# Local attention on TensorE: the value projection moved directly behind the output projection, the transposed inverses behind the scores

## The chip, the cores and the metric

The kernel is one program on one core of a Trainium2 chip. Its engines run their own instruction queues side by side and meet through semaphores: TensorE (matrix products and transposes into PSUM), VectorE (DVE), ScalarE (ACT), GpSimd (POOL) and SyncE (SP), which only issues DMAs here. The metric is the device time in microseconds (us); lower is better. PSUM has 8 banks of 512 fp32 columns per partition, and this kernel uses all of them in local attention.

## The reference

The input is 4 x 512 x 256 x 4 image values and 4 x 512 x 256 text values. An embedding reduces the image to 4 x 512 x 256 and the text is put behind it: 4096 rows of 256. Then comes a layer of linear attention with 16 heads, and then twice a layer of local attention and a gated MLP:

```
h = shift_token(x); q, k, v = split(h @ wqkv)          # 8 heads of 64
q = l2norm(q) * qs; k = l2norm(k) * ksc; q, k = rotary_xpos(q, k)
sim = 8 * q_window @ [k_previous_window, k_window]^T   # windows of 128 rows
attn = softmax(masked sim); o = attn @ [v_previous, v]
x = x + o @ wo                                         # and then the MLP
```

All of it is fp32. The change lies in this part, which runs twice (`local_phase`, `layer` 0 and 1).

## The kernel before

**Windows and stages.** The 4096 rows are 32 windows of 128 (`T`). `schedule` calls `step(n, r, a, b, c, d)` for n = 0 to 34 on each of TensorE, ScalarE and VectorE. Steps 0 to 3 and 32 to 34 are written out; steps 4 to 31 are a hardware loop over pairs of steps (`r` is 0 and 1). Each step works on up to four windows at once: flag `a` is the q and k projection of window n and the input of window n+1, `b` and the scores belong to window n-1, `c` (probabilities transposed, values) to window n-2, `d` (output projection) to window n-3. The order inside a queue is the order of the calls, written out by hand: nothing is reordered.

**Precision.** Projections are three fp32r matmuls, high times high, high times low and low times high (`matmul3`, lines 116 to 118). Operands come as a high part copied by ScalarE and a low part subtracted by VectorE. Transposes are matmuls by the identity.

**TensorE, a step.** `project` of q and k (12 matmuls of 512 columns, L116 to L118); 8 transposes of the rotated q and k (L1170), which wait for `rotated` of POOL; `probs_t` for pairs of heads 0 and 1 (L1133); the output projection (12 matmuls of 256 columns), which waits for `o_done`; `probs_t` for pairs 2 and 3; `project` of v (6 matmuls); `x_t` (L1107, two transposes of the next input); `inverses` (L1152, four transposes of the spread reciprocal row sums); `score` twice (L1126, 16 matmuls); `values` (L1143, 32 matmuls).

**Banks.** `QK, V, TQ, OT = 0, 2, 3, 7`: q and k in banks 0 and 1, v in 2, transposed q and k in 3 and 4, outputs in 7. Scores take banks 0, 1, 3 and 4 again. `XT, RB = 5, 6` and `PT = (5, 6, 5, 6)`: `x_t` shares bank 5 with pairs 0 and 2, `inverses` share bank 6 with pairs 1 and 3. So `x_t` waits for ScalarE's copy of pair 2 (`p_done`), and `inverses` for that of pair 3.

**ScalarE, a step** (L916 to L948): high part of the last output (L920), copy of v (L924), squares of q and k (L928), copies of transposed q and k (L932), four copies of transposed probabilities (`probs_out`, L914), high part of the next x (L896), the input copies (L888 or L889), the copy of the transposed inverses (L945, waits for `r_t`), then the exponentials (L908, eight for a window, each pair waits for `masked`). In the loop there is also one piece of the MLP's weights before each pair of steps (L954).

**VectorE, a step** (L1010 to L1068): in every second step the mask (L1013), the reciprocal of the row sums (L1018, waits for `exped`), the low part of the output (L1022), the rotation (L1030, L1035, waits for `squared`), the residual (L1042), the sums of squares (L1044), small steps for the norm (L998 to L1006), the low part of x (L980, L982), the eight score reductions with mask (L989, wait for `scored`) with more of the small steps between them, and the product of values and inverses (L1068).

**GpSimd**: the sum of the rotated halves (L862), the product by the norm (L866, raises `rotated`), one piece of the MLP's weights in every second step (L876), and the spread of the inverses (L854).

Of the kernel before, what the change touches and what calls it, by code (L numbers as in the profile page):

```python
# [89 lines left out]
class Chain:  # L90
# [16 lines left out]
    def wait(self):  # L107
        self.eng.wait_ge(self.sem, self.base + self.n)
# [5 lines left out]
def matmul3(nc, out, wh, wl, mh, ml, start, stop):  # L114

    nc.tensor.matmul(out, wh, mh, start=start, stop=False, skip_group_check=True)  # L116
    nc.tensor.matmul(out, wh, ml, start=False, stop=False, skip_group_check=True)  # L117
    return nc.tensor.matmul(out, wl, mh, start=False, stop=stop, skip_group_check=True)  # L118
# [646 lines left out]
def local_phase(nc, s, mem, K, A, layer):  # L765
# [29 lines left out]
    QK, V, TQ, OT = 0, 2, 3, 7  # L795
# [17 lines left out]
    with nc.Block() as block:  # L813

        @block.sync
        def _(sp):
            sp.dma_start(flags[:], A.flags).then_inc(s.const_in.sem, 16)
            if layer == 0:
                for dst, src in K.local_loads(layer):
                    sp.dma_start(dst, src).then_inc(K.local_in.sem, 16)  # L820
            for dst, src in ((cos[:], A.rope_cos), (sin[:], A.rope_sin), (prev[:], A.mask_prev),
                             (mask_o[:, P:2 * P], A.mask_cur), (mask_e[:, 0:P], A.mask_cur),
                             (mask_o[:, 0:P], A.mask_prev), (negs[:], A.negs),
                             (qks[:, 0, :], A.ffn_q_scale[layer:layer + 1].to_broadcast([P, DH])),
                             (qks[:, 1, :], A.ffn_k_scale[layer:layer + 1].to_broadcast([P, DH]))):
                sp.dma_start(dst, src).then_inc(s.const_in.sem, 16)
            sp.wait_ge(*s.padded.after(1))
            for dst, src in K.mlp_loads(layer):
                sp.dma_start(dst, src).then_inc(K.mlp_in.sem, 16)
            with sp.Fori(0, T // 2) as p:  # L830
                for r in range(2):
                    sp.wait_ge(*s.y_done.after(2 * p + r + 1))
                    sp.wait_ge(*K.rows_stored[r].after(16 * (layer * T // 2 + p)))
                    sp.dma_start(A.scratch[bass.ds((2 * p + r) * P + 1, P), :].rearrange("(o p) c -> p o c", o=1),
                                 X[:, bass.ds(2 * p + r, 1), P:D]).then_inc(K.rows_stored[r].sem, 16)

            sp.wait_ge(*K.mlp_in.after(16 * len(K.mlp_loads(layer)) * (layer + 1)))
# [264 lines left out]
        @block.tensor  # L1102
        def _(pe):
            def x_t(t, r):
                wait(pe, s.x_copied, t + 1)
                for c in range(KC):
                    last = nc.tensor.transpose(ps[:, XT, c * P:(c + 1) * P],  # L1107
                                               xc[:, r, c * P:(c + 1) * P], K.ident[:])
                last.then_inc(s.x_t.sem, 1)

            def project(r, w, bank):

                cols = slice(w * LINNER, (w + 1) * LINNER)
                for c in range(KC):
                    at = XW * c - c
                    last = matmul3(nc, ps[:, bank], xt[:, r, 0, at:at + P], xt[:, r, 1, at:at + P],
                                   wh[:, c, cols], wl[:, c, cols], c == 0, c == KC - 1)
                return last

            def score(half):  # L1120

                bank = QK if half == 0 else TQ
                for pair in (2 * half, 2 * half + 1):
                    for e in range(2):
                        rows, at = slice(e * DH, (e + 1) * DH), pair % 2 * 2 * P
                        last = nc.tensor.matmul(ps[:, bank + e, at:at + 2 * P], qt[rows, pair, :],  # L1126
                                                kt[rows, :, pair, :], start=True, stop=True)
                last.then_inc(s.scored.sem, 1)

            def probs_t(t, pair):  # L1130
                wait(pe, s.exped, 4 * t + pair + 1)
                for k in range(4):
                    last = nc.tensor.transpose(ps[:, PT[pair], k * P:(k + 1) * P],  # L1133
                                               pm[:, pair, k * P:(k + 1) * P], K.ident[:])
                last.then_inc(s.p_t.sem, 1)

            def values():

                for pair in range(LPAIRS):
                    for w in range(2):  # L1140
                        for e in range(2):
                            h = 2 * pair + e
                            last = nc.tensor.matmul(ps[e * DH:(e + 1) * DH, OT, pair * P:(pair + 1) * P],  # L1143
                                                    vv[:, w, h * DH:(h + 1) * DH],
                                                    pt[:, pair, (2 * e + w) * P:(2 * e + w + 1) * P],
                                                    start=(w == 0), stop=(w == 1))
                last.then_inc(s.o_full.sem, 1)

            def inverses():

                for pair in range(LPAIRS):
                    last = nc.tensor.transpose(ps[:, RB, pair * P:(pair + 1) * P],  # L1152
                                               spread[:, pair * P:(pair + 1) * P],
                                               K.ident[:])
                last.then_inc(s.r_t.sem, 1)

            def step(n, r, a, b, c, d):
                if a or b:
                    wait(pe, s.x_done, n + 1)
                if a:  # L1160
                    wait(pe, s.turned, n)
                    wait(pe, s.masked, 4 * (n - 1) - 2)
                    project(r, 0, QK)
                    project(r, 1, QK + 1).then_inc(s.qk_full.sem, 1)
                if b:
                    wait(pe, s.rotated, n)
                    wait(pe, s.masked, 4 * (n - 1))
                    for k in range(2):
                        for m in range(LPAIRS):
                            last = nc.tensor.transpose(ps[:, TQ + k, m * P:(m + 1) * P], t1[:, k, m * P:(m + 1) * P],  # L1170
                                                       K.ident[:])
                        last.then_inc(s.qk_t.sem, 1)
                if c:
                    probs_t(n - 2, 0)
                    wait(pe, s.r_out, n - 2)
                    probs_t(n - 2, 1)
                if d:
                    wait(pe, s.o_done, n - 2)
                    for m in range(LPAIRS):
                        cols = slice(m * P, (m + 1) * P)  # L1180
                        last = matmul3(nc, ps[:, OT, 0:D], oth[:, cols], otl[:, cols], woh[:, m, :], wol[:, m, :],
                                       m == 0, m == LPAIRS - 1)
                    last.then_inc(s.y_full.sem, 1)
                if c:
                    for pair in (2, 3):
                        wait(pe, s.p_done, 4 * (n - 2) + pair - 1)
                        probs_t(n - 2, pair)
                if b:
                    wait(pe, s.v_done, n - 1)
                    project(1 - r, 2, V).then_inc(s.v_full.sem, 1)  # L1190
                if a:
                    if c:
                        wait(pe, s.p_done, 4 * (n - 2) + 3)
                    x_t(n + 1, 1 - r)
                if c:
                    wait(pe, s.spread, n - 1)
                    wait(pe, s.p_done, 4 * (n - 1))
                    inverses()
                if b:
                    wait(pe, s.qk_done, 2 * n)  # L1200
                    if a:
                        wait(pe, s.turned, n + 1)
                    score(0)
                    score(1)
                if c:
                    wait(pe, s.v_done, n - 1)
                    wait(pe, s.y_done, n - 2)
                    values()

            x_t(0, 0)  # L1210
            if layer == 0:
                pe.wait_ge(*s.w_lo.after(len(PIECES)))
            schedule(pe, step)


# [578 lines left out]
```

## Time and profile before

| | |
|---|---|
| time, median of 3 runs | 2147.8 us (2147.47 to 2151.69) |
| profiled execution | 2146.89 us, its span 2145.1 us |
| TensorE matmuls busy | 1979.4 us (92%) |
| VectorE busy | 1547.7 us (72%) |
| ScalarE busy | 1088.3 us (51%) |
| GpSimd busy | 435.6 us (20%) |
| two windows in layer 0, 1000.30 to 1026.80 | TensorE busy 26.21 us of 26.50, VectorE 24.09, ScalarE 22.05 |

Local attention lies between about 780 and 1240 us (layer 0) and between about 1450 and 1920 us (layer 1). Times in the rows below are microseconds from the start of the span. In a timeline, a row gives the start, the duration, the engine, the line, the operation with its output and inputs, and in brackets the idle time before it with what ended it; neighbours of one kind are merged (x8). Matmuls overlap: their starts tell when the engine takes them, while their durations reach into the next one.

### The profile page before, as it was taken

What the parts mean: (1) busy time and instruction counts of PE and PEld (TensorE: products, weight loads), DVE (VectorE), ACT (ScalarE), POOL (GpSimd) and SP (SyncE); (2) the same over time, 40 slices, a digit from 0 to 9 for tenths busy, and PEclk for the clock granted to TensorE, in tenths of its full rate; (3) what the DMA queues carried; (4) which work ended last, traced back from release to release, by engine and by line L of the source; (5) the groups of instructions that cost most, each with busy time, mean ns of one, the idle gap of its engine ahead of it and who ended that gap; (6) DMA issues with size and microseconds to landing.
All of it is one profiled execution on the core that took longest, in us unless ns stands there. A gap on an engine that the chain in (4) does not pass through costs nothing. (4 is left out here: it accounts for less than half of the span.)

```text
span 2145.1 us, 42708 instructions
## 1 busy us (share of the span) xinstructions
PE 1979.4 (92%) x13792; PEld 1692.4 (79%) x13792; DVE 1547.7 (72%) x4590; ACT 1088.3 (51%) x2517; POOL 435.6 (20%) x265
## 2 busy tenths in 40 slices
PE   8799999899999959999999879995999999959998
PEld 8688788788878847888888668884888888857887
DVE  7356546546636668999998677775899999957777
ACT  5322232232222228888888624443777777743433
POOL 3100000000000014444444200002444444420010
PEclk9899999999999979999999989997999999989999
DMA  8000000000000020000000010001000000000002
GB/s 300 1 1 1 2 1 1 2 1 1 1 2 1 1 105 5 5 5 5 5 5 5 5 61 11 15 5 65 6 5 5 5 5 5 5 16 15 11 10 83
DMA packets 43179, 42.20 MB, mean 20 GB/s; under 512 B 8552, under 2 KB 37959, under 8 KB 43080
## 3 DMA queue, kind: packets, MB, share of 16 engines
q1 hardware_dynamic: 43080, 40.90, 5.8%
q8 instruction: 60, 0.98, 0.2%
q14 instruction: 39, 0.32, 0.0%
HBM read 32.49 MB, written 8.39 MB: 19 GB/s over the span
## 5 line engine op out<-in xcount | busy, mean ns | idle before, releaser
L908 ACT ACTIVATE l_probs<-l_probs,l_negmax 128x256 f32<-128x256 f32 x512 | 253.2, 496 | 65.1 <-DVE l_negmax L989 65.1
L116 PE MATMUL ps<-local_w_hi,l_xT 128*128 128x512 f32 x384 | 167.9, 437 | 37.1 <-DVE l_xT L982 31.2
L862 POOL TENSOR_TENSOR l_t<-l_t,l_t 128x1024 f32<-128x1024 f32 x64 | 152.9, 2388 | 196.3 <-DVE l_t L1035 196.3
L116 PE MATMUL ps<-attn_w_hi,attn_xT_hi 128*128 128x512 f32 x392 | 169.3, 432 | 18.5 <-issue 10.0
L866 POOL TENSOR_TENSOR l_t<-l_t,l_rnorm 128x1024 f32<-128x1024 f32 x64 | 121.9, 1905 | 307.9 <-DVE l_rnorm L1006 307.9
L419 ACT ACTIVATE attn_exp<-ps 128x512 f32<-128x512 f32 x130 | 77.6, 598 | 209.9 <-PE ps L118 209.9
L914 ACT ACTIVATE l_probsT<-ps 128x512 f32<-128x512 f32 x256 | 138.3, 594 | 49.5 <-PE ps L1133 49.5
L117 PE MATMUL ps<-attn_w_lo,attn_xT_hi 128*128 128x512 f32 x392 | 158.5, 404 | 0.0
L118 PE MATMUL ps<-attn_w_hi,attn_xT_lo 128*128 128x512 f32 x392 | 158.0, 403 | 0.0
L510 DVE TENSOR_SCALAR attn_exp<-attn_exp 128x512 f32<-128x512 f32 x130 | 58.8, 453 | 136.6 <-ACT attn_exp L419 136.5
L118 PE MATMUL ps<-local_w_hi,l_xT 128*128 128x512 f32 x384 | 155.4, 405 | 0.0
L117 PE MATMUL ps<-local_w_lo,l_xT 128*128 128x512 f32 x384 | 155.2, 404 | 0.0
L116 PE MATMUL ps<-m_hnT_hi,ffn_w_hi 128*128 128x512 f32 (+1 forms) x352 | 143.1, 407 | 4.6 <-DVE m_hnT_lo L1372 4.6
L117 PE MATMUL ps<-m_hnT_lo,ffn_w_hi 128*128 128x512 f32 (+1 forms) x352 | 140.2, 398 | 0.0
L118 PE MATMUL ps<-m_hnT_hi,ffn_w_lo 128*128 128x512 f32 (+1 forms) x352 | 140.2, 398 | 0.0
L842 POOL MEMSET ffn_w_raw<- 128x44 f32 x2 | 0.3, 136 | 686.6 <-POOLq L384 684.7
L1133 PE MATMUL ps<-ident,l_probs 128*128 128x128 f32 x1024 | 133.9, 274 | 1.7 <-ACT l_probsT L914 1.7
L1126 PE MATMUL ps<-l_kT,l_qT 64*128 64x256 f32 x1024 | 127.9, 389 | 2.5 <-DVE l_t L1035 2.5
L1143 PEld LDWEIGHTS ps<-l_probsT,l_v 128*64 128x64 f32 x2048 | 110.5, 137 | 20.9 <-issue 20.9
L1143 PE MATMUL ps<-l_probsT,l_v 128*64 128x128 f32 x2048 | 125.9, 276 | 0.0
L116 PEld LDWEIGHTS ps<-local_w_hi,l_xT 128*128 128x128 f32 x384 | 74.8, 195 | 61.2 <-DVE l_xT L982 23.8
L1317 ACT ACTIVATE m_gelu<-ps,ffn_b 128x512 f32<-128x512 f32 x80 | 55.0, 688 | 127.7 <-PE ps L118 127.7
(210 smaller groups left out, 5832.2 us busy)
## 6 DMA issues: line engine op xcount, KB each, us to landing
tok_x<-x SPq DMA_DIRECT2D x16, 512.0 KB, 5.6
m_shifted<-shifted SPq DMA_DIRECT2D x20, 256.0 KB, 2.7
shifted<-x SPq DMA_DIRECT2D x64, 64.0 KB, 1.5
out<-x SPq DMA_DIRECT2D x8, 512.0 KB, 4.4
ffn_w_raw<-ffn_w SPq DMA_DIRECT2D x6, 640.0 KB
local_w_raw<-ffn_wqkv SPq DMA_DIRECT2D x4, 768.0 KB, 5.3
h<-txt SPq DMA_DIRECT2D x4, 512.0 KB, 9.6
attn_w_raw<-attn_Wk SPq DMA_DIRECT2D x1, 1024.0 KB, 7.5
```

What stands on the lines that cost most here:

```text
L116: nc.tensor.matmul(out, wh, mh, start=start, stop=False, skip_group_check=True)
L117: nc.tensor.matmul(out, wh, ml, start=False, stop=False, skip_group_check=True)
L118: return nc.tensor.matmul(out, wl, mh, start=False, stop=stop, skip_group_check=True)
L419: nc.scalar.activation(ex[:, at % 2], ps[:, at % 2], ACT.Exp).then_inc(s.attn_exp.sem, 1)
L510: chain(nc.vector.tensor_scalar(ex[:, at % 2], ex[:, at % 2], 1.0, None, ALU.min))
L862: nc.gpsimd.tensor_tensor(t1[:], t1[:], t2[:], ALU.add).then_inc(s.summed.sem, 1)
L866: nc.gpsimd.tensor_tensor(r, r, rn[:].unsqueeze(2).to_broadcast([P, 2 * LH, DH]), ALU.mult).then_inc(s.rotated.sem, 1)
L908: last = nc.scalar.activation(v, v, ACT.Exp, bias=nb[:, h:h + 1], scale=-1.0, accum_out=rsum[:, h:h + 1])
L914: nc.scalar.activation(pt[:, pair], ps[:, PT[pair]], ACT.Copy).then_inc(s.p_done.sem, 1)
L1126: last = nc.tensor.matmul(ps[:, bank + e, at:at + 2 * P], qt[rows, pair, :], kt[rows, :, pair, :], start=True, stop=True)
L1133: last = nc.tensor.transpose(ps[:, PT[pair], k * P:(k + 1) * P], pm[:, pair, k * P:(k + 1) * P], K.ident[:])
L1143: last = nc.tensor.matmul(ps[e * DH:(e + 1) * DH, OT, pair * P:(pair + 1) * P], vv[:, w, h * DH:(h + 1) * DH], pt[:, pair, (2 * e + w) * P ...
```

## The change

In a step of TensorE two blocks move. The wait for `v_done` and the projection of v come directly behind the output projection, ahead of `probs_t` for pairs 2 and 3. The inverses, with their two waits, come behind the two `score` calls, directly ahead of `values`. The other engines' code is as before.

```
                     last.then_inc(s.y_full.sem, 1)
+                if b:
+                    wait(pe, s.v_done, n - 1)
+                    project(1 - r, 2, V).then_inc(s.v_full.sem, 1)
                 if c:
                     for pair in (2, 3):
                         wait(pe, s.p_done, 4 * (n - 2) + pair - 1)
                         probs_t(n - 2, pair)
-                if b:
-                    wait(pe, s.v_done, n - 1)
-                    project(1 - r, 2, V).then_inc(s.v_full.sem, 1)
                 if a:
                     if c:
                         wait(pe, s.p_done, 4 * (n - 2) + 3)
                     x_t(n + 1, 1 - r)
-                if c:
-                    wait(pe, s.spread, n - 1)
-                    wait(pe, s.p_done, 4 * (n - 1))
-                    inverses()
                 if b:
                     wait(pe, s.qk_done, 2 * n)
                     if a:
...
                     score(0)
                     score(1)
                 if c:
+                    wait(pe, s.spread, n - 1)
+                    wait(pe, s.p_done, 4 * (n - 1))
+                    inverses()
                     wait(pe, s.v_done, n - 1)
                     wait(pe, s.y_done, n - 2)
                     values()
```

## Rows read from the trace of the kernel before

**Rows 1.** Stretch of two windows: PE, PEld, DVE, ACT, POOL busy, PEclk, DMA, GB/s.
```profile
1598.53:1625.02 26.49, 26.19 (x219) 22.24 (x217) 24.05 (x80) 20.63 (x58) 11.84 (x7) 1.00 0.02 5
```

**Rows 2.** Waits, 1510 to 1880 us: total us, times, longest.
```profile
PEld ps L1170 <- POOL l_t L866: 16.4, 28, 0.8
```

**Rows 3.** Timeline of TensorE (PE) over two windows of layer 1.
```profile
1594.70 2.00 PE L1126 MATMUL ps<-l_kT,l_qT 64*128 64x256 f32 x16
...
1607.95 2.00 PE L1126 MATMUL ps<-l_kT,l_qT 64*128 64x256 f32 x16
1609.87 1.97 PE L1143 MATMUL ps<-l_probsT,l_v 128*64 128x128 f32 x32
1611.77 0.50 PE L116 MATMUL ps<-local_w_hi,l_xT 128*128 128x512 f32 x1
...
1614.40 0.40 PE L118 MATMUL ps<-local_w_hi,l_xT 128*128 128x512 f32 x1
1614.96 1.09 PE L1170 MATMUL ps<-ident,l_t 128*128 128x128 f32 x8 [0.16 <-POOL l_t L866]
...
1616.68 0.36 PE L116 MATMUL ps<-local_w_hi,l_oT_hi 128*128 128x256 f32 x1
...
1618.18 1.04 PE L1133 MATMUL ps<-ident,l_probs 128*128 128x128 f32 x8
1618.97 0.47 PE L116 MATMUL ps<-local_w_hi,l_xT 128*128 128x512 f32 x1
...
1620.45 0.38 PE L1107 MATMUL ps<-ident,l_x 128*128 128x128 f32 x2
1620.66 0.60 PE L1152 MATMUL ps<-ident,l_spread 128*128 128x128 f32 x4
1621.19 2.00 PE L1126 MATMUL ps<-l_kT,l_qT 64*128 64x256 f32 x16
```

**Rows 4.** Timeline of ScalarE (ACT) in the same windows.
```profile
1596.78 0.51 ACT L908 ACTIVATE l_probs<-l_probs,l_negmax 128x256 f32<-128x256 f32 x1 [1.24 <-DVE l_negmax L989]
...
1600.73 0.45 ACT L954 ACTIVATE ffn_w_hi<-ffn_w_raw  x1
...
1602.08 1.01 ACT L928 ACTIVATE l_sq<-ps 128x1024 f32<-128x1024 f32 x1
...
1610.03 0.51 ACT L908 ACTIVATE l_probs<-l_probs,l_negmax 128x256 f32<-128x256 f32 x1 [1.24 <-DVE l_negmax L989]
...
1618.81 1.09 ACT L914 ACTIVATE l_probsT<-ps 128x512 f32<-128x512 f32 x2 [0.91 <-PE ps L1133]
```

**Rows 5.** The page's groups: busy us, mean ns of one, idle before.
```profile
L914 ACT ACTIVATE l_probsT<-ps 128x512 f32<-128x512 f32 x256 | 138.3, 594 | 49.5 <-PE ps L1133 49.5
```

**Rows 6.** Timeline of VectorE (DVE) in the same windows.
```profile
1601.82 1.38 DVE L1022 TENSOR_TENSOR l_oT_lo<-l_oT,l_oT_hi 128x512 fp32r<-128x512 f32 x1 [0.67 <-ACT l_oT_hi L920]
1603.39 1.22 DVE L1030 TENSOR_TENSOR l_t<-ps,l_cos 128x1024 f32<-128x1024 f32 x1 [0.19 <-issue]
...
1609.14 0.42 DVE L989 CUSTOM_DVE_ANT_0 l_probs<-ps,l_mask_odd 128x256 f32<-128x256 f32 x1
...
1616.28 1.23 DVE L1030 TENSOR_TENSOR l_t<-ps,l_cos 128x1024 f32<-128x1024 f32 x1
```

**Rows 7.** Timeline of GpSimd (POOL) in the same windows.
```profile
1613.00 1.91 POOL L866 TENSOR_TENSOR l_t<-l_t,l_rnorm 128x1024 f32<-128x1024 f32 x1 [4.72 <-DVE l_rnorm L1006]
```

**Rows 8.** Timeline of TensorE in the first windows of layer 0.
```profile
805.93 0.62 PE L116 MATMUL ps<-local_w_hi,l_xT 128*128 128x512 f32 x1 [2.98 <-DVE l_negmax L989]
806.35 0.63 PE L117 MATMUL ps<-local_w_lo,l_xT 128*128 128x512 f32 x1
...
813.09 1.15 PE L1133 MATMUL ps<-ident,l_probs 128*128 128x128 f32 x8 [0.84 <-ACT l_probsT L914]
```

**Rows 9.** Timeline of TensorE and ScalarE in the run-out of layer 1.
```profile
1898.22 0.60 PE L1152 MATMUL ps<-ident,l_spread 128*128 128x128 f32 x4
...
1898.85 0.60 ACT L945 ACTIVATE l_oT<-ps 128x512 f32<-128x512 f32 x1 [1.17 <-PE ps L1152]
```

More of the change, by code:

```diff
@@ L1183, in step @@
                     last.then_inc(s.y_full.sem, 1)
+                if b:
+                    wait(pe, s.v_done, n - 1)
+                    project(1 - r, 2, V).then_inc(s.v_full.sem, 1)
                 if c:
@@ L1187, in step @@
                         probs_t(n - 2, pair)
-                if b:
-                    wait(pe, s.v_done, n - 1)
-                    project(1 - r, 2, V).then_inc(s.v_full.sem, 1)
                 if a:
@@ L1194, in step @@
                     x_t(n + 1, 1 - r)
[L1195 to L1198, printed above, removed]
                 if b:
@@ L1205, in step @@
                 if c:
+                    wait(pe, s.spread, n - 1)
+                    wait(pe, s.p_done, 4 * (n - 1))
+                    inverses()
                     wait(pe, s.v_done, n - 1)
```

## The prediction

> **What bounds the kernel now.** I read the busy rows of stretches first, then the waits, then the timelines of all engines over two consecutive windows of local attention, since the change touches only `local_phase`. In the steady part TensorE is busy 26.19 us of 26.49, at a granted clock of 1.00, and no wait of any size stands before its matmuls [rows 1]. That looks like a stage bound by TensorE alone. It isn't quite: the weight loads of the transposes of q and k (L1170) wait for POOL's `l_t` (L866) in all 28 windows, 0.59 us each [rows 2]. The timeline says what that costs: the last matmul of the q and k projections starts at 1614.40, its neighbours are 0.23 apart, so the next could start at 1614.63, and it starts at 1614.96 [rows 3]. So 0.33 us in each window is lost, and another chain closes the period at the same 13.24 us (scores at 1594.70, 1607.95 and 1621.19 [rows 3]).
>
> That chain can be followed over two windows, from the scores at 1594.70 to those at 1621.19:
> - scores start 1594.70 to first exponential 1596.78 (ACT L908, after the first masks on DVE): 2.08 [rows 3, 4].
> - exponentials, the ffn piece (L954, once in two windows), `oT_hi`, the copy of v, and the squares: 1596.78 to DVE's rotation (L1030) at 1603.39: 6.61. The squares start at 1602.08 and take 1.01, so the rotation starts 0.30 behind their end [rows 4, 6].
> - rotation to first masks (L989) at 1609.14: 5.75 [rows 6]. DVE has no idle time in it.
> - masks, with the rnorm steps between them, then POOL L866 from 1613.00 for 1.91, then the transposes of q and k at 1614.96: 5.82 [rows 3, 6, 7].
> - transposes to scores at 1621.19: 6.23 of TensorE's own work [rows 3].
>
> The sum is 26.49, exactly the two periods. ScalarE's exponentials are therefore on the bounding chain, though ScalarE itself is not full. The other interleaved chain (from the scores at 1607.95) has no ffn piece: first exponential 1610.03 to rotation 1616.28 is 6.25 [rows 4, 6]; the 0.36 between the two is the ffn piece. It is a little shorter and waits for the first one.
>
> **The change, part by part.** No instruction is added or removed and no DMA moves; two blocks of TensorE move in each window. SP's queue is not passed, POOL's is touched only through `r_t`.
>
> 1. *Value projection before the last two `probs_t`.* Its 6 matmuls take 1.48 us (1618.97 to 1620.45). What they need, ScalarE's copy of the last v, is done with the L924 copy ahead of the squares at 1602.08, long before. In the steady part no stall stands before `probs_t` 2 now (12 matmuls of the output projection, 1616.68 to 1618.18, then directly on), so nothing is gained there. But the projection now lies between `probs_t` 2, 3 and `x_t`, and hides a wait: `x_t` writes bank 5, which pair 2's probabilities use (`PT`), so it waits for ScalarE's copy of pair 2. After the move `x_t` is directly behind the transposes. `probs_t` 2 starts at 1618.18, ScalarE starts the copy at 1618.81 (0.63 later) and two copies take 1.09, one 0.594 in the mean, so what is behind a copy starts 0.50 after it [rows 3 to 5]; with 0.07 for the signal (POOL's end at 1614.91 to 1614.96 is 0.05; I add a little) `x_t` can start 1.29 behind `probs_t` 2. The transposes themselves take 0.79 (1618.18 to 1618.97). New stall: 0.50 per window. Bounds: nothing, if the copy needed only the time of the transposes; 0.84, the stall that the first full window shows between these very transposes when ScalarE is late [rows 8]. I take 0.50, as ScalarE would be idle and ready.
>
> 2. *Inverses behind the scores.* On TensorE they take 0.53 (1620.66 to 1621.19) in either place. They free the scores by 0.53, which the stall of 0.50 eats. Their wait for pair 3's copy is now hidden behind the scores (1.92, 1607.95 to 1609.87). But ScalarE's program is unchanged: `on` is copied out of the bank of the inverses *before* the exponentials, in the same queue. Queued behind that waiting copy are the eight exponentials, and behind these all of the chain above. Now the copy is done when the masks are; after the change the inverses start 1.92 behind the scores, where the values start now (1607.95 to 1609.87 [rows 3]), the copy starts 0.63 behind them (1898.22 to 1898.85, in the run-out, where ScalarE waits for exactly this [rows 9]), and the next instruction 0.50 later. First exponential: 1.92 + 0.63 + 0.50 = 3.05 behind the scores, not 2.08. That is 0.97 on the chain. Bounds: 0.47 (if the copy's 0.50 were free) and 1.5 (if a whole block of the 0.53 inverses came on top).
>
> 3. *Transposes to scores.* Before 6.23. After: 1.72 to the output projection (1614.96 to 1616.68), 1.50 for it, 1.48 for v, 0.79 for the transposes, 0.50 stall, 0.21 for `x_t` (1620.45 to 1620.66): 6.20. No change worth naming (-0.03).
>
> The chain over two windows becomes 26.49 + 0.97 - 0.03 = 27.43, or 13.71 each. TensorE alone would need 13.24 - 0.33 + 0.50 = 13.41, less than that, so the chain sets the period. The old stall of 0.33 at L1170 goes where the chain leaves room and comes back in every other window. The output projection is a second new wait: it needs `oT_lo`, which in the ffn window ended at 1603.20 [rows 6] against a start of the projection 1.72 behind the transposes, about 0.2 of slack; with `oT_hi` 0.97 later that slack is gone and up to 0.6 of stall appears in that window. The windows share the same two-window sum, so it moves idle time between them and does not add.
>
> Sum: the loop has 28 windows in each of two layers, 28 pairs in all: 28 x 0.94 = 26.3 us. Edges: the first full window gains about 1.2 on TensorE (the 0.84 stall [rows 8] goes behind the value projection, the inverses go), most of which the later exponentials take back; the run-out pays the late exponential once more, about 0.4 a layer. Together +0.7. Against the profiled execution's 2146.89 (span 2145.1 and 1.8 around it) this gives 2146.9 + 27.0 = 2173.9; the median of the runs is 0.9 above the profiled one, well inside their spread. I predict 2174.
>
> A word on the clock. In the trace a stall of 2.98 us ahead of the projections at 805.93 is followed by matmuls 0.42 apart, the lower of TensorE's two levels (1.2 GHz), against 0.23 at the upper (2.4 GHz) [rows 8]; steady windows, with their 0.33, stay at 1.00 [rows 1]. This is the row's answer: the new 0.5 us stalls cost only themselves.
>
> The Trainium skill, page "TensorE: Matmul & The Clock Gate", section "A second HAM failure mode: psum-queue depth-cycling", says that frequent micro-idles between groups of matmuls can make the clock oscillate even without one long gap. By that rule the new stalls could pull the clock down in every window; no row here shows it. The mechanism and its time stand with the rivals, from rows.
>
> **The rivals.**
> - *TensorE and the bank wait alone* (the late exponentials are absorbed by slack that the timeline hides, for instance if the 0.30 between squares and rotation shrinks and DVE's steps run faster without POOL beside them). Period 13.41: 56 x 0.17 = 9.5, so 2157. Against it: the chain adds up to the measured period without a remainder.
> - *`oT_lo` becomes serial too.* If its 1.38 form (POOL's spreading beside it) appears in both windows, each output projection waits. From scores to scores with the ffn piece: 3.05, then 6.42 from the first exponential (1596.78) to the end of `oT_lo` (1603.20 [rows 4, 6]), 0.07 for the signal and 4.48 from the output projection on (step 3 without its first 1.72) make 14.02; without the piece 0.36 less, 13.66. Two windows 27.68, +1.19, 28 x 1.19 = 33: with the edges 2181.
> - *Faster.* One mechanism: the wait for POOL at L1170 is what the old order pays, and the new order fills it, since the inverses now lie between the scores and the projections, 0.53 more TensorE work ahead of the transposes. If ScalarE's early copy of pair 2 and the exponentials fit, the period is 13.24 - 0.33 = 12.91: 56 x -0.33 = -18, 2129. It decides if the stall before `x_t` stays under 0.33 and the first exponential within 0.3 of its present place. Both are refused by the order on ScalarE.
> - *The clock falls* with two short stalls a window instead of one. If the 12 projection matmuls a window ran 0.42 apart, not 0.23: +2.3 a window, 56 x 2.3 = 129, 2146.9 + 129 + 27 = about 2303. Against it: 1.00 in the steady windows, with a stall in each [rows 1, 2].
> - *It does nothing measurable*: late and early effects cancel to within 0.08 us a window; nothing in the rows leads there.
>
> **How the numbers follow.** Forecast 0.68 (2166 to 2182 by itself); bank wait alone 0.14; serial `oT_lo` 0.09; clock 0.02; nothing 0.03; faster 0.04. The ends of the bounds give 2159 (no stall before `x_t`: 0.50 off the chain, 28 x 0.44 = 12) and 2188 (late exponentials at 1.5: 28 x 1.47 = 41); with the first rival's 2157 the range is 2155 to 2188. A change of under 0.2% (4.3 us) can't be told from none here; slower than that is 0.93, within it 0.03, faster 0.04.
>
> **What would show it.** In the changed kernel's steady windows: idle time of some 0.5 us before L1107, put down to ScalarE's L914; ScalarE's L945 waiting for L1152 in every window, and L908 following L945 directly, with its wait for DVE's L989 gone; first exponential 3.05 behind the scores; two windows 27.4 long. DVE's L1030 waits for the squares. Step 2 is wrong if L908 still waits for the masks; step 1 is wrong if L1107 follows L1133 with no gap; the whole is wrong if the period stays under 13.4 while both are seen.

## The result, and the profile after

The changed kernel takes 2179.47 us (median of 4, 2178.97 to 2180.87) against 2148.78 before (2147.47 to 2151.69): a ratio of 1.0142, 95% interval 1.0124 to 1.0160. Forecast was 2174 within 2155 to 2188, slower by more than 0.2% with a chance of 0.93. Its profiled execution took 2179.78, the span 2178.0, which is 32.9 more than before.

Two windows of the changed kernel, then its waits in 1515 to 1880 us, which answer to [rows 1] and [rows 2] (columns as there; the stretch has 27 of its windows):

```profile
1612.74:1640.26 27.52, 26.87 (x217) 22.21 (x216) 23.48 (x80) 20.64 (x57) 11.85 (x8) 1.00 0.02 5
```

```profile
ACT l_oT L945 <- PE ps L1152: 49.3, 27, 1.8
...
DVE l_t L1030 <- ACT l_sq L928: 16.0, 26, 0.7
...
PE ps L1107 <- ACT l_probsT L914: 8.7, 27, 0.3
...
PEld ps L1170 <- POOL l_t L866: 6.1, 19, 0.7
```

One more wait of the kernel before, in 1510 to 1880 us (28 windows):

```profile
ACT l_probs L908 <- DVE l_negmax L989: 34.9, 28, 1.4
```

Two windows take 27.52 us instead of 26.49, at the same granted clock. The wait for POOL's `l_t` shrank from 16.4 to 6.1 us, and three waits are new: ScalarE's copy of the transposed inverses (L945) waits for TensorE in every window, VectorE's rotation (L1030) waits for the squares, and `x_t` (L1107) for the copy of pair 2. ScalarE's 34.9 us of waiting for the masks are gone: L908 follows L945 without a gap.

TensorE's timeline, answering to [rows 3]:

```profile
1612.74 2.00 PE L1126 MATMUL ps<-l_kT,l_qT 64*128 64x256 f32 x16
1614.66 0.66 PE L1152 MATMUL ps<-ident,l_spread 128*128 128x128 f32 x4
...
1620.91 1.04 PE L1133 MATMUL ps<-ident,l_probs 128*128 128x128 f32 x8
1621.93 0.38 PE L116 MATMUL ps<-local_w_hi,l_oT_hi 128*128 128x256 f32 x1
...
1626.54 2.00 PE L1126 MATMUL ps<-l_kT,l_qT 64*128 64x256 f32 x16
...
1633.92 1.09 PE L1170 MATMUL ps<-ident,l_t 128*128 128x128 f32 x8
...
1638.54 1.03 PE L1133 MATMUL ps<-ident,l_probs 128*128 128x128 f32 x8
1639.90 0.43 PE L1107 MATMUL ps<-ident,l_x 128*128 128x128 f32 x2 [0.33 <-ACT l_probsT L914]
1640.26 2.00 PE L1126 MATMUL ps<-l_kT,l_qT 64*128 64x256 f32 x16
```

ScalarE's, then VectorE's, in the same windows, answering to [rows 4] and [rows 6]:

```profile
1615.36 0.60 ACT L945 ACTIVATE l_oT<-ps 128x512 f32<-128x512 f32 x1 [1.82 <-PE ps L1152]
1615.85 0.50 ACT L908 ACTIVATE l_probs<-l_probs,l_negmax 128x256 f32<-128x256 f32 x1
...
1621.14 1.01 ACT L928 ACTIVATE l_sq<-ps 128x1024 f32<-128x1024 f32 x1
```

```profile
1622.45 1.23 DVE L1030 TENSOR_TENSOR l_t<-ps,l_cos 128x1024 f32<-128x1024 f32 x1 [0.58 <-ACT l_sq L928]
...
1628.10 0.42 DVE L989 CUSTOM_DVE_ANT_0 l_probs<-ps,l_mask_odd 128x256 f32<-128x256 f32 x1
```

The chain of the prediction can be read off again, as stretches between starts: scores 1612.74, first exponential 1615.85 (3.11), rotation 1622.45 (6.60), masks 1628.10 (5.65), transposes of q and k 1633.92 (5.82), scores 1640.26 (6.34). The sum is 27.52, the two periods without a remainder.

For all kernels below, the time is split by the starts of the score blocks (L1126): *run-in* is from the first to the third, *loop* the 28 windows behind it, given for two windows, *run-out* from the last block of the loop to the start of the last three matmuls of the last output projection. Each is given for layer 0 / layer 1, from the timeline of one profiled execution of each kernel, so it can differ by a few us from what the median execution would show. The ratio is to the kernel before, measured beside it.

| kernel | loop, two windows | run-in | run-out | median us | ratio, 95% |
|---|---|---|---|---|---|
| before | 26.49 / 26.47 | 28.5 / 28.5 | 31.7 / 31.0 | 2148.8 to 2150.3 | |
| changed | 27.51 / 27.53 | 27.5 / 28.2 | 34.3 / 34.8 | 2179.5 | 1.0142 (1.0124 to 1.0160) |
| v_alone | 28.11 / 28.09 | 28.4 / 29.0 | 34.3 / 34.7 | 2199.6 | 1.0231 (1.0212 to 1.0249) |
| inv_alone | 26.99 / 27.00 | 28.1 / 27.7 | 35.3 / 38.6 | 2169.2 | 1.0086 (1.0070 to 1.0103) |
| v_moved_inv_mid | 27.52 / 27.52 | 28.2 / 28.2 | 31.7 / 31.7 | 2176.9 | 1.0123 (1.0105 to 1.0142) |
| inv_mid | 26.47 / 26.43 | 28.1 / 28.0 | 30.8 / 30.6 | 2146.1 | 0.9988 (0.9974 to 1.0003) |
| after_copy_mid | 27.17 / 27.15 | 28.1 / 28.2 | 32.7 / 35.4 | 2169.4 | 1.0084 (1.0067 to 1.0101) |
| inv_alone_copy_mid | 27.09 / 26.99 | 27.2 / 27.8 | 38.1 / 33.6 | 2165.8 | 1.0073 (1.0057 to 1.0089) |
| inv_alone_copy_mid_sq | 26.63 / 26.57 | 27.2 / 27.2 | 31.3 / 35.4 | 2152.9 | 1.0017 (1.0006 to 1.0028) |
| after_busy_runout | 27.50 / 27.51 | 27.5 / 28.2 | 31.7 / 31.5 | 2174.2 | 1.0119 (1.0102 to 1.0135) |
| inv_alone_busy_runout | 26.99 / 27.00 | 27.1 / 28.1 | 31.6 / 31.5 | 2158.5 | 1.0047 (1.0033 to 1.0060) |
| inv_mid_busy_runout | 26.45 / 26.45 | 27.7 / 27.1 | 30.5 / 30.5 | 2141.3 | 0.9966 (0.9952 to 0.9979) |

### The profile page after: what moved, and what is told of

Read it like the earlier page. It is cut to its first block and busy times, and to the rows that moved or that the text cites. A ratio compares the mean times of both kernels' runs of the same rounds, so it can differ in the third digit from the quotient of the medians.

```text
span 2178.0 us, 42708 instructions
## 1 busy us (share of the span) xinstructions
PE 2002.4 (92%) x13792; PEld 1694.0 (78%) x13792; DVE 1534.9 (70%) x4590; ACT 1088.6 (50%) x2517; POOL 434.5 (20%) x265
## 5 line engine op out<-in xcount | busy, mean ns | idle before, releaser
L908 ACT ACTIVATE l_probs<-l_probs,l_negmax 128x256 f32<-128x256 f32 x512 | 252.5, 498 | 6.9 <-DVE l_negmax L989 6.9
L116 PE MATMUL ps<-local_w_hi,l_xT 128*128 128x512 f32 x384 | 162.7, 424 | 36.8 <-DVE l_xT L982 30.8
L118 PE MATMUL ps<-local_w_hi,l_xT 128*128 128x512 f32 x384 | 155.2, 404 | 0.0
L1126 PE MATMUL ps<-l_kT,l_qT 64*128 64x256 f32 x1024 | 127.8, 389 | 2.3 <-DVE l_t L1035 2.3
L1133 PEld LDWEIGHTS ps<-ident,l_probs 128*128 128x128 f32 x1024 | 120.4, 143 | 9.5 <-issue 0.9
L1030 DVE TENSOR_TENSOR l_t<-ps,l_cos 128x1024 f32<-128x1024 f32 x64 | 78.4, 1224 | 57.5 <-ACT l_sq L928 55.8
```

What stands on the lines that cost most here:

```text
L908: last = nc.scalar.activation(v, v, ACT.Exp, bias=nb[:, h:h + 1], scale=-1.0, accum_out=rsum[:, h:h + 1])
L1030: nc.vector.tensor_tensor(t1[:].rearrange("p a (h d) -> p a h d", d=DH), q, cw, ALU.mult)
```

## The experiments

Theory: two waits were made, the bank wait ahead of `x_t` by the first move and the late exponentials by the second, and the second sets the period through ScalarE. Rivals: only one of the two costs.

**v_alone** does the first move alone.

```
                     last.then_inc(s.y_full.sem, 1)
+                if b:
+                    wait(pe, s.v_done, n - 1)
+                    project(1 - r, 2, V).then_inc(s.v_full.sem, 1)
                 if c:
                     for pair in (2, 3):
...
-                if b:
-                    wait(pe, s.v_done, n - 1)
-                    project(1 - r, 2, V).then_inc(s.v_full.sem, 1)
```

> Half of the change alone: the value projection directly behind the output projection, the inverses still ahead of the scores. Own theory: the exponentials start where they did before (2.1 us behind the scores), so all that is new is the bank wait ahead of x_t, 0.57 us, and a slow start of x_t behind it, 0.16 (both as the changed kernel shows them). TensorE alone then needs 12.91 + 0.73 = 13.64 us a window, 27.28 for two, while the chain over ScalarE would need 26.49 + 0.73 - 0.10 = 27.12. TensorE sets the period, +0.79 for two windows, 28 x 0.79 = +22: about 2171. Rival A (only the late exponentials cost, the bank wait is covered by the wait for POOL that goes away): 2149, no change. Rival B (only the bank wait costs): 2171 too, but then the other half alone is faster than before.

It came out at 2199.6, worse than both moves together, and 28 us above the highest of the three forecasts. The timelines of TensorE and of VectorE, then two waits in 1515 to 1880 us (26 windows):

```profile
1606.44 1.03 PE L1133 MATMUL ps<-ident,l_probs 128*128 128x128 f32 x8
1607.80 0.43 PE L1107 MATMUL ps<-ident,l_x 128*128 128x128 f32 x2 [0.33 <-ACT l_probsT L914]
1608.31 0.63 PE L1152 MATMUL ps<-ident,l_spread 128*128 128x128 f32 x4
1608.86 2.00 PE L1126 MATMUL ps<-l_kT,l_qT 64*128 64x256 f32 x16
...
1615.88 1.09 PE L1170 MATMUL ps<-ident,l_t 128*128 128x128 f32 x8 [0.16 <-POOL l_t L866]
...
1622.91 2.00 PE L1126 MATMUL ps<-l_kT,l_qT 64*128 64x256 f32 x16
```

```profile
1610.06 0.42 DVE L989 CUSTOM_DVE_ANT_0 l_probs<-ps,l_mask_odd 128x256 f32<-128x256 f32 x1 [0.81 <-issue]
```

```profile
DVE l_probs L989 <- issue: 19.2, 24, 0.8
PEld ps L1170 <- POOL l_t L866: 14.8, 26, 0.7
```

The bank wait is there as forecast (1607.80 is 1.36 behind 1606.44). But one window is a closed loop of its own: scores 1608.86 to masks 1610.06 (1.20), masks to transposes 1615.88 (5.82), transposes to scores 1622.91 (7.03), 14.05 in all, the period. Neither ScalarE's exponentials nor TensorE's total work is in it: TensorE still waits for POOL in every window, and VectorE now stands idle ahead of the first mask. The profile names no engine for that idle time; that it ends with the scores is read from the distance, 1.20 here and 1.19 before. I had not seen that loop. It was in the rows of before as well: 1.19 from scores to masks, 5.82, 6.23 [rows 3, 6] make 13.24, the same number as half the two-window chain. So before, two loops were tied. The first move lengthens the stretch from transposes to scores by 0.80, and the one-window loop pays it in every window, 56 x 0.8 = 45; that is the loops' part of the loss (2 x 22.7 in the table's figures). So the bank wait does cost, as my theory and rival B had it, but through a loop that none of the three forecasts contained, and all three (2171, 2149, 2171) are out. Whether it is the only cost is judged by the next kernel.

**inv_alone** does the second move alone.

```
-                if c:
-                    wait(pe, s.spread, n - 1)
-                    wait(pe, s.p_done, 4 * (n - 1))
-                    inverses()
...
                     score(1)
                 if c:
+                    wait(pe, s.spread, n - 1)
+                    wait(pe, s.p_done, 4 * (n - 1))
+                    inverses()
                     wait(pe, s.v_done, n - 1)
```

> The other half alone: the inverses behind the scores, the value projection where it was, so x_t has no bank wait. Own theory: the first exponential starts 3.11 us behind the scores, because ScalarE's copy of the inverses stands ahead of the exponentials in its queue; the scores start 0.53 earlier. Chain for two windows: 3.11 + 6.60 + 5.70 + 5.82 + 5.70 = 26.93, against 26.49 before: 28 x 0.44 = +12, about 2161, with TensorE idle some 0.5 us a window ahead of the transposes of q and k. Rival B (TensorE and its bank wait alone decide): TensorE needs 12.91 a window, 28 x (25.82 - 26.49) = -19, about 2130. Rival A (late exponentials make all of the changed kernel's loss): 2179.

Measured 2169.2 where the theory had 2161; the loops are 27.00, where it had 26.93 and rival B 25.82. TensorE's timeline, then one row of ScalarE's:

```profile
1604.92 2.00 PE L1126 MATMUL ps<-l_kT,l_qT 64*128 64x256 f32 x16
...
1618.25 0.38 PE L1107 MATMUL ps<-ident,l_x 128*128 128x128 f32 x2
1618.56 2.00 PE L1126 MATMUL ps<-l_kT,l_qT 64*128 64x256 f32 x16
...
1626.14 1.09 PE L1170 MATMUL ps<-ident,l_t 128*128 128x128 f32 x8
...
1631.94 2.00 PE L1126 MATMUL ps<-l_kT,l_qT 64*128 64x256 f32 x16
```

```profile
1607.55 0.60 ACT L945 ACTIVATE l_oT<-ps 128x512 f32<-128x512 f32 x1 [1.83 <-PE ps L1152]
```

ScalarE sits idle for 1.83 us, waiting for the inverses, and the exponentials queue behind. TensorE's stretch from transposes to scores is short here (5.80, 1626.14 to 1631.94), so the one-window loop (1.19 + 5.82 + 5.80 = 12.81) is far below the period, and the chain over ScalarE sets it: this move loses without any bank wait. Rivals A and B are both out. The loops lose 2 x 7.3 us; the other 9 of the 23.7 by which its span is longer lie outside them: the run-outs are 11 longer, the rest 2 shorter. The theory did not have the run-outs.

**v_moved_inv_mid** and **inv_mid** put the inverses between the two halves of the scores, with the value projection moved and not moved.

```
                     score(0)
+                if c:
+                    wait(pe, s.spread, n - 1)
+                    wait(pe, s.p_done, 4 * (n - 1))
+                    inverses()
+                if b:
                     score(1)
```

(The inverses' other place goes.)

> The changed kernel with the inverses between the two halves of the scores, so that ScalarE's copy of them (from 1.6 us behind the start of the scores) is done when the first masks are, and the exponentials start 2.1 behind the scores again. Own theory: the chain falls to 27.52 - 1.01 = 26.5 for two windows, but TensorE still has the bank wait and needs 13.66 a window, 27.3: 0.2 less than the changed kernel, 28 x 0.2 = 6, about 2173, with no wait of the rotation for the squares. Rival A (late exponentials are the whole loss): about 2151. Rival B: no change against the changed kernel, 2179.

> The value projection where it was, the inverses between the two halves of the scores: neither the bank wait nor the late exponentials. Own theory: scores 0.53 earlier behind the transposes (5.70 instead of 6.23), first exponential 2.1 behind the scores: 25.98 over TensorE's chain. A loop of VectorE and ScalarE alone takes over: 12.96 in the window with the mask (VectorE has no gap in it) and 0.89 + 6.60 + 5.75 = 13.24 in the other, 26.20 for two windows, -0.29, 28 x -0.29 = -8: about 2140, faster than before. Rival B: TensorE's 12.91 a window, 2130. Rival (the split costs more on TensorE than it gives, second half of the scores too late for the masks): 2149 or more.

The first has loops of 27.52, where 27.3 was forecast; the second 26.45, where 26.2 was forecast. The timeline of inv_mid, then its row for two windows:

```profile
1603.04 0.38 PE L1107 MATMUL ps<-ident,l_x 128*128 128x128 f32 x2
1603.35 1.13 PE L1126 MATMUL ps<-l_kT,l_qT 64*128 64x256 f32 x8
1604.41 0.66 PE L1152 MATMUL ps<-ident,l_spread 128*128 128x128 f32 x4
1605.00 1.14 PE L1126 MATMUL ps<-l_kT,l_qT 64*128 64x256 f32 x8
1606.06 1.97 PE L1143 MATMUL ps<-l_probsT,l_v 128*64 128x128 f32 x32
```

```profile
1603.35:1629.80 26.45, 26.45 (x218) 22.16 (x217) 23.90 (x80) 21.05 (x57) 11.84 (x8) 1.00 0.02 5
```

Half of the scores takes 1.06 before the next block starts, not 0.96, and the inverses 0.59 instead of 0.53: the split costs 0.26 us of TensorE. The step from `x_t` straight to the scores adds 0.10 (0.31 instead of the 0.21 that `x_t` took ahead of the inverses). TensorE is then busy 26.45 of 26.45 us. So inv_mid is bound by TensorE, at 13.2 a window and not at the 12.91 that I had worked out (12.91 + 0.26 + 0.10 = 13.27), and the loop gains next to nothing. At 2146.1 it met none of its forecasts (2140, 2130, 2149 or more), and the interval of its ratio includes 1. It does show that both waits are avoidable at once: ScalarE's copy ends when the masks are ready, and there is no bank wait.

That v_moved_inv_mid has the changed kernel's 27.52 is a coincidence of two limits, as one wait in 1515 to 1880 us shows, here for v_moved_inv_mid:

```profile
PEld ps L1170 <- POOL l_t L866: 0.5, 1, 0.5
```

TensorE waits for POOL in one window, against 19 times in the changed kernel: here its own work, the split and the bank wait fill the period. Rival A (2151) is out. The time of 2176.9 alone does not separate my 2173 from rival B's 2179, nor did the rotation's wait for the squares go away, as I had expected. The next kernel separates them.

**after_copy_mid** leaves the changed kernel's TensorE as it is and moves the copy on ScalarE.

```
                 if b:
-                    for pair in range(LPAIRS):
+                    for pair in range(2):
                         exps(n - 1, pair)
+                if c:
+                    wait(act, s.r_t, n - 1)
+                    wait(act, s.o_done, n - 2)
+                    nc.scalar.activation(on[:], ps[:, RB], ACT.Copy).then_inc(s.r_out.sem, 1)
+                if b:
+                    for pair in range(2, LPAIRS):
+                        exps(n - 1, pair)
```

(The same copy ahead of the exponentials goes.)

> The changed kernel's order on TensorE; on ScalarE the copy of the transposed inverses (L945) stands between the exponentials of pair 1 and pair 2 instead of ahead of all eight. Own theory: exponentials start 2.1 us behind the scores and the last ends 0.5 earlier than in the changed kernel, so the two-window chain falls from 27.52 to 27.0; TensorE with its bank wait needs 7.30 from scores to transposes and 6.28 back, 13.58 a window, 27.16 for two, and sets the period: 28 x (27.16 - 27.52) = -10 against the changed kernel, 2169. Rival (TensorE alone sets the changed kernel's period): no change, 2179. The run-out stalls before the transposes fall with the earlier exponentials, another -2 to -5 if the clock then stays up.

Measured 2169.4, loops of 27.17 and 27.15 where 27.16 was forecast. Its row for two windows, and one wait in 1515 to 1880 us (the edit adds three lines, so that L1170 is L1173 in the kernels with it, L1126 is L1129 and L989 is L992):

```profile
1607.00:1634.17 27.17, 26.52 (x219) 22.31 (x218) 23.63 (x80) 20.62 (x57) 11.92 (x8) 1.00 0.02 5
```

```profile
PEld ps L1173 <- POOL l_t L866: 1.1, 2, 0.7
```

Only ScalarE's order was changed, so on top of what TensorE with the bank wait takes the late exponentials cost 0.36 for two windows in the changed kernel, about 10 of its 31 us. What is left is TensorE with the bank wait: it waits for POOL in 2 windows only. The rival is out. The further gain in the run-outs did not come: 32.7 and 35.4, against 34.3 and 34.8.

**inv_alone_copy_mid** does the same on top of inv_alone, and **inv_alone_copy_mid_sq** also swaps two of ScalarE's instructions:

```
-                if c:
-                    wait(act, s.v_full, n - 1)
...
                 if a:
                     wait(act, s.qk_full, n + 1)
...
+                if c:
+                    wait(act, s.v_full, n - 1)
```

> The inverses behind the scores, the value projection where it was, and ScalarE's copy of the inverses between the exponentials of pair 1 and 2. Own theory: two-window chain 27.00 - 0.50 = 26.50 as measured periods go, against 26.48 before: no difference in the loop. Run-outs as before where the clock stays at 1.00: 2149 in all, 20 less than with the copy ahead of the exponentials. Rival (the late inverses cost by something else than ScalarE's queue, TensorE's switches between transposes and scores): 2165 to 2169.

> As inv_alone_copy_mid, and ScalarE takes the squares of q and k (L928) ahead of the copy of v (L924), so that the rotation on VectorE can start up to 0.48 us earlier. Own theory: the chain loses 0.3 to 0.4 over two windows and meets TensorE (2 x 13.0) and the loop of VectorE and ScalarE at 26.2: 28 x -0.28 = -8, about 2141, faster than before. Rival (the squares now wait for the projections of q and k, which end at 7.5 behind the scores, so nothing is gained): 2149.

The first missed: the loops stay at 27.0, and 2165.8 was measured where 2149 was forecast. That time lies in the rival's range, but not for the rival's reason, as will be seen. TensorE's scores, then ScalarE's first exponential:

```profile
1611.00 2.00 PE L1129 MATMUL ps<-l_kT,l_qT 64*128 64x256 f32 x16
```

```profile
1613.65 0.51 ACT L908 ACTIVATE l_probs<-l_probs,l_negmax 128x256 f32<-128x256 f32 x1 [1.86 <-DVE l_negmax L992]
...
1618.44 0.62 ACT L920 ACTIVATE l_oT_hi<-l_oT 128x512 fp32r<-128x512 f32 x1
```

The exponentials start 2.65 behind the scores, not 2.1, because VectorE is now the one that comes late with the masks (1.86 us of ScalarE's idle time are put down to it). From there the half microsecond of the copy is in the way: what goes from masks over exponentials to squares and back to masks never passes TensorE, and the copy is inside that loop wherever it stands behind the first exponential. Before, it was done while ScalarE waited for masks, and cost nothing. So what counts is not when the exponentials start but whether the copy is finished before the masks come. The swap of the squares, which touches ScalarE's queue alone, takes 0.4 off the same loop (27.04 to 26.60 in the mean): the gain forecast, from a start that was 0.5 higher than I thought. So the loop was held by ScalarE's queue and not by TensorE. The time, 2152.9, is 12 above the 2141 forecast.

**after_busy_runout** and, from it, **inv_alone_busy_runout** and **inv_mid_busy_runout** test the run-outs. Each adds surplus projections where TensorE would wait.

```
+                if a is False and b:
+                    wait(pe, s.masked, 4 * (n - 1) - 2)
+                    project(r, 0, QK)
+                    project(r, 1, QK + 1)
                 if b:
                     wait(pe, s.rotated, n)
...
+                if c and not b:
+                    wait(pe, s.masked, 4 * (n - 1))
+                    project(r, 0, QK)
+                    project(r, 1, QK + 1)
                 if d:
                     wait(pe, s.o_done, n - 2)
```

> The changed kernel with surplus work: in the first two steps of the run-out, where no window is left to project, TensorE runs the 12 matmuls of the q and k projection once more while it would wait (results unused). Theory (the run-out's extra time, 2.7 us in layer 0 and 3.8 in layer 1 over the kernel before, is partly TensorE's clock, granted at 0.77 and 0.74 behind the idle stretches of 2.7 to 3.2 us): the clock stays at 1.00, the surplus lies in idle time, and the run-outs are 1 to 3 shorter each, 2175. Rival (the clock has nothing to do with the idle stretch): surplus work costs nothing or up to 2 us, 2179 to 2181, and the clock falls as before.

> The inverses behind the scores, the value projection where it was, and surplus work in the run-out: in its first two steps TensorE runs the 12 matmuls of the q and k projection once more while it would wait (results unused). Theory (inv_alone loses 14.5 us in its loops and some 11 in its run-outs, 35.3 and 38.6 us against 31.7 and 31.0 before, most of it TensorE's granted clock of 0.5 to 0.7 there): clock 1.00 in the run-outs, each some 31.7 long, 10 less in all: about 2159, the loops unchanged at 27.0 for two windows. Rival (the run-outs are longer because the exponentials are late, not because of the clock): run-outs of 34 to 36 and 2165 or more.

> The inverses between the two halves of the scores (loop of 26.45 for two windows against 26.48 before), and the same surplus work in the run-out. There the clock was at 1.00 without it, with run-outs of 30.8 and 30.6 us. Theory: nothing to win, 2146, run-outs within 0.5 of that; the surplus itself is free. If the surplus has a cost of its own it shows here as 1 to 3 us, and has to be taken off what it gave in the other two kernels.

The run-outs came out as the theory has it in all three: 31.7 and 31.5, 31.6 and 31.5, 30.5 and 30.5. So did the times of the first two (2175 and 2159 forecast); the third took 2141.3 where 2146 was forecast. Stretches of the changed kernel's run-out in layer 1, and of after_busy_runout's (columns as in [rows 1]; the number behind the last bracket is the granted clock):

```profile
1915.46:1922.50 7.04, 4.48 (x53) 3.60 (x52) 5.52 (x32) 5.11 (x19) 2.33 (x2) 1.00 0.00 0
1922.50:1929.81 7.31, 7.15 (x42) 6.69 (x43) 2.04 (x3) 3.50 (x9) 1.10 (x2) 0.77 0.04 11
1929.81:1939.00 9.19, 5.72 (x62) 4.47 (x61) 5.28 (x21) 7.24 (x23) 1.04 (x1) 0.91 0.00 1
1939.00:1949.10 10.10, 7.14 (x56) 6.36 (x57) 1.81 (x3) 2.42 (x4) 0.00 (x0) 0.74 0.03 8
```

```profile
1915.00:1923.00 8.00, 8.00 (x73) 6.87 (x71) 4.99 (x23) 7.45 (x23) 2.95 (x2) 1.00 0.01 2
1923.00:1930.00 7.00, 7.00 (x70) 5.88 (x70) 3.28 (x18) 2.65 (x8) 0.00 (x0) 1.00 0.03 9
1930.00:1939.00 9.00, 7.47 (x52) 5.85 (x50) 2.85 (x6) 6.01 (x19) 1.04 (x1) 1.00 0.03 8
```

And the whole run-outs of the kernel before, then those of inv_mid_busy_runout:

```profile
1200.25:1231.89 31.64, 22.31 (x216) 19.41 (x216) 13.53 (x58) 18.74 (x53) 4.38 (x3) 0.95 0.02 5
1885.72:1916.76 31.04, 21.65 (x216) 18.93 (x216) 13.58 (x59) 17.95 (x52) 4.39 (x4) 0.98 0.02 6
```

```profile
1198.12:1228.61 30.49, 27.48 (x244) 22.83 (x244) 14.35 (x59) 18.96 (x53) 5.05 (x4) 1.00 0.02 6
1879.92:1910.42 30.50, 27.49 (x245) 22.90 (x245) 14.26 (x59) 18.28 (x52) 5.05 (x4) 1.00 0.02 6
```

More work, less time: with matmuls that only keep TensorE busy the clock stays at 0.99 and 1.00 over the changed kernel's run-outs (0.90 and 0.85 without them) and at 1.00 over inv_alone's (0.85 and 0.76). The changed kernel wins 5.3 us (2179.5 to 2174.2), inv_alone 10.7 (2169.2 to 2158.5). **inv_mid_busy_runout** is the only kernel here that beats the one before beyond its interval, 0.9966 (0.9952 to 0.9979), and beats the changed one by 38 us. In the profiled executions its gain is 6.6 us: 0.8 in the loops, 2.1 in the run-ins, 1.7 in the run-outs, and 2.0 in parts that no edit touches.

## Why the prediction was right, and where it was off

- *The chain over ScalarE sets the period* (step 2): right. It closes at 27.52 against 27.43 forecast, L945 waits in every window, and after_copy_mid, which shortens that chain alone, shortens the period. By less than the prediction's numbers give, though: they put the chain 0.61 above TensorE alone for two windows (27.43 against 2 x 13.41), and 0.36 was measured, as TensorE with the bank wait needs 27.16.
- *Scores to first exponential*: 3.05 forecast, 3.11 measured.
- *Bank wait ahead of `x_t`* (step 1): 1.29 behind `probs_t` forecast (0.63 + 0.594 for the copy of pair 2 + 0.07; the 0.50 that the prediction names beside it is when ScalarE's next copy starts), 1.36 measured (1638.54 to 1639.90), a stall of 0.57 instead of 0.50.
- *Transposes to scores* (step 3): 6.20 forecast, 6.34 measured. 0.07 is the stall, and `x_t` then takes 0.36 to the scores instead of 0.21; in inv_alone, without a stall, it takes 0.31 (1618.25 to 1618.56), so most of that is the step from `x_t` straight to the scores, which the old order did not have.
- *Rotation to masks*: 5.75 taken as it was, 5.65 measured.
- *Output projection waits for `oT_lo` in one window of two*: right. 1620.91 to 1621.93 is 1.02 for a block that takes 0.79, a stall of 0.23 where up to 0.6 was allowed for; with the two-window sum as it is, it does not add.
- *The sum*: loops 28 x 0.94 = 26.3 forecast, 14.3 + 14.9 = 29.2 measured. Edges +0.7 forecast, +5.2 measured: run-ins -1.2, run-outs +6.4. The parts that the change does not touch were 1.5 shorter in this execution, which is luck. 29.2 + 5.2 - 1.5 = 32.9.

The term that was most mis-sized is the run-outs: forecast 0.4 a layer, measured 2.7 and 3.8. With the clock held up by surplus work they are 31.7 and 31.5, so 2.6 and 3.3 of them go with the clock, a term that the prediction did not have. That leaves 0.0 and 0.4 over the kernel before, but its run-outs were partly at the lower clock too (0.95 and 0.98), and it was not run with surplus work. The late exponentials alone show between two kernels at 1.00: inv_alone_busy_runout and inv_mid_busy_runout differ only in the place of the inverses and in their run-outs by 1.1 and 1.0. So the 0.4 for them was also too small. "TensorE alone 13.41" was 13.58 by after_copy_mid.

One loop was missing from the working, that of one window over the masks. It does not bind in the changed kernel (1.19 + 5.82 + 6.34 = 13.35, under 13.76), because the second move takes the inverses' 0.53 out of the stretch into which the first puts the bank wait. So the forecast of both moves together came out, and the same working failed by 28 us on the first move alone. That the missing loop did not bind here was luck: nothing in the prediction excludes it. The first move alone costs 50 us; the second, by itself a loss of 20, takes 20 of them away.

Of the clock: the steady windows have the new stalls and are at 1.00, in the two windows above and over all of 1530 to 1912 us, so the fourth rival is out for the loop. The run-out of layer 1, in which TensorE idles 2.73 and 3.22 us, shows 0.77 and 0.74. The rule of the Trainium skill that was weighed in the prediction ("TensorE: Matmul & The Clock Gate", "A second HAM failure mode: psum-queue depth-cycling") does not show in these loops.

## What to carry to other kernels

When an engine looks full, write down every closed loop that passes it, over one step and over two, with and without each other engine: here two loops were equal to 0.01 us, and each move of a block lengthened or shortened them by different amounts, so that the halves of a change did not add up. A block that is moved behind another on the producing engine delays the first consumer and all that is queued behind that consumer; it is free only if the consumer had been idle anyway. Before moving a block, ask which wait it was hiding.

## What the runs showed of the hardware

- TensorE's clock at the end of a phase is worth microseconds even if the phase's loop is at full speed. Nearly the same idle stretches did not give the same clock: with 3.16 and 3.22 us in layer 1 the kernel before had 1.00 behind the second one (1906.95 to 1910.30), with 3.16 and 3.21 us in layer 0 it had 0.63 there (1221.48 to 1226.05), and the changed kernel with 2.73 and 3.22 us in layer 1 fell to 0.77 and 0.74. inv_mid's 12 times reach from 2140.4 to 2153.1, while with the surplus matmuls its 5 times lie between 2140.3 and 2144.5. Over the 12, time and the clock granted in the whole span go together, from 2140.4 us at 0.972 to 2153.1 us at 0.964; in which stretches the slower ones lost their clock was not traced. The Trainium skill, page "TensorE: Matmul & The Clock Gate", section "What's actually happening", says of a kernel's start that the number of matmuls at the lower clock varies from run to run. The spread here is of that kind, but no run shows that it has the same cause.
- Breaking a block of scores (64 rows used) by a block of transposes (128 rows) cost TensorE 0.26 us: 1.06 for half the scores instead of 0.96, twice, and 0.59 for the inverses instead of 0.53. That the different number of rows is the reason was not tested.
